# Attention plus RWKV-style FFN on 8 cores: x + attention on VectorE alone, r products moved earlier, matmuls on idle data ahead of the FFN

## The reference

```python
# x: (4, 4096, 1024) fp32; LN is layernorm without scale or shift
z = LN(x);  q, k, v = z @ Wq, z @ Wk, z @ Wv            # D = 64
att = softmax(q @ k.T, axis=1)                          # over the queries
x = x + tile(att @ v, 16)                               # the 64 columns repeated 16 times
z = LN(x);  z_prev = z shifted by one token
xr = mu_r * z + (1 - mu_r) * z_prev;  xk = mu_k * z + (1 - mu_k) * z_prev
r = sigmoid(xr @ W_r.T);  ka = square(relu(xk @ W_k.T))
x = x + r * (ka @ W_v.T)                                # W_r, W_k, W_v: 1024 x 1024
```

## Time and profile before

| | |
|---|---|
| median of 3 runs | 395.83 us (395.75 to 396.2) |
| the profiled execution | 396.79 us, span of its slowest core (core 0) 394.9 us |
| spans of the 8 cores | 388.7 to 394.9 us |
| busy: PE, DVE, ACT, POOL | 79%, 57%, 57%, 29% of the span |
| chain that ended last, by engine | PE 52%, ACT 20%, DVE 12%, issue 11% |
| costliest groups of that chain | V products (L1080) 14%, r products (L1037) 10%, keys (L1058) 10% |

### The profile page before, as it was taken

The page is one execution under the profiler, slowest core; times in us unless marked ns, Lnnn a source line. Parts: engine busy times, 40 slices in busy tenths (PEclk is TensorE's granted clock), DMA queues, the critical chain, the costliest instruction groups (busy, mean ns, idle before and its releaser), DMA issues.

```text
span 394.9 us, 6253 instructions; the slowest of 8 cores (388.7 to 394.9 us)
## 1 busy us (share of the span) xinstructions
PE 312.6 (79%) x1938; PEld 143.1 (36%) x1938; DVE 224.5 (57%) x440; ACT 225.9 (57%) x354; POOL 116.5 (29%) x161
## 2 busy tenths in 40 slices
PE   0377986696878767776526989799999999999994
PEld 0333332231224434342223334244444444444441
DVE  2787789337236631112188976879278836781045
ACT  1252289989889999999916409302860267014610
POOL 1887457607304885068470021001000000000000
PEclk9997798866695888886555989899999999999999
DMA  7999547896596789991002004131322214130014
GB/s 179 291 317 287 144 140 188 147 290 102 101 173 188 250 176 181 183 266 79 1 2 46 7 2 81 27 147 67 55 53 106 110 33 75 69 144 2 0 53 160
DMA packets 42368, 48.58 MB, mean 123 GB/s; under 512 B 33248, under 2 KB 33504, under 8 KB 41952
## 3 DMA queue, kind: packets, MB, share of 16 engines
q1 hardware_dynamic: 41472, 41.44, 37.5%
q0 software_dynamic: 864, 6.75, 10.7%
HBM read 38.68 MB, written 8.39 MB: 119 GB/s over the span
## 4 chain that ended last, share of the span: by engine, by line
PE 52%; ACT 20%; DVE 12%; issue 11%; DMA 2%; POOL 1%; DVEq 0%; SPq 0%; ACTq 0%; POOLq 0%
PE F L1080 14%; PE F L1037 10%; PE F L1058 10%; PE tf L827 6%; PE F L886 6%; ACT Prot L1139 5%; ACT junkL L1139 5%; ACT junk L1139 4%; ACT P L1139 3%; DMA xst<-x_in 2%; DVE xr L667 2%; PE acc L899 2%; PE tf L863 1%; PE tx L810 1%; DVE dxk L677 1%
## 5 line engine op out<-in xcount | busy, mean ns | idle before, releaser
L886 PE MATMUL F<-qk 64*128 64x512 bf16 x136 | 59.2, 456 | 34.4 <-ACT Prot L1139 11.0
L1058 PE MATMUL F<-dxk,wk 128*128 128x512 bf16 x256 | 58.6, 386 | 1.8 <-DVE dxk L677 1.7
L1080 PE MATMUL F<-wv,ka 128*128 128x512 bf16 x256 | 57.5, 387 | 2.9 <-ACT ka L1186 2.9
L1178 ACT ACTIVATE rr<-F 128x1024 bf16<-128x1024 f32 x16 | 16.4, 1023 | 73.6 <-PE F L1037 73.6
L1037 PE MATMUL F<-wr,xr 128*128 128x512 bf16 x256 | 57.8, 384 | 0.6 <-DVE xr L667 0.6
L890 PE MATMUL F<-qk 64*128 64x512 bf16 x120 | 54.8, 474 | 0.0
L1139 ACT ACTIVATE P<-F,negm 128x1024 bf16<-128x1024 f32 (+1 forms) x40 | 37.2, 948 | 19.5 <-PE F L886 15.6
L1139 ACT ACTIVATE junk<-F,negm 128x1024 bf16<-128x1024 f32 x32 | 39.8, 1255 | 3.1 <-PE F L890 3.1
L1139 ACT ACTIVATE junkL<-F,negm 128x1024 bf16<-128x1024 f32 x32 | 39.9, 1281 | 0.0
L417 POOL TENSOR_SCALAR zst<-xst,nmean,rstd 128x1024 bf16<-128x1024 f32 x32 | 38.0, 1194 | 3.6 <-POOL rstd L407 3.6
L1139 ACT ACTIVATE Prot<-F,negm 128x1024 bf16<-128x1024 f32 x32 | 39.0, 1346 | 0.0
(11 more groups left out here) (103 smaller groups left out, 446.7 us busy)
## 6 DMA issues: line engine op xcount, KB each, us to landing
xst<-x_in SPq DMA_DIRECT2D x32, 512.0 KB, 7.1
x<-x_in SPq DMA_DIRECT2D x16, 512.0 KB, 5.3
y_out<-x SPq DMA_DIRECT2D x15, 512.0 KB, 2.6
wr<-wr_in POOLq DMA_DIRECT2D x1, 2048.0 KB, 16.2
wk<-wk_in POOLq DMA_DIRECT2D x1, 2048.0 KB, 18.2
wv<-wv_in POOLq DMA_DIRECT2D x1, 2048.0 KB, 21.0
y_out<-x SPq DMA_DIRECT2D x2, 256.0 KB, 2.1
wqk<-wqk_in POOLq DMA_DIRECT2D x1, 256.0 KB, 9.2
```

Of the source, the lines that this page charges most:

```text
L886: t.matmul(f[:, 0:512], qk2[0:64, kt * 128:(kt + 1) * 128], qk1[0:64, i0:i0 + 512], start=True, stop=True, skip_group_check=True, tile_pos ...
L1058: ins = t.matmul(F[k_ % 3][:, dd * 512:(dd + 1) * 512], wk[:, ct, dt * 128:(dt + 1) * 128], dxk[:, q % 2, ct, :], start=(ct == 0), stop=(c ...
L1080: ins = t.matmul(F[(8 + j) % 3][:, hh * 512:(hh + 1) * 512], ka[:, dt, j * 128:(j + 1) * 128], wv2[:, dt, hh * 512:(hh + 1) * 512], start= ...
```

## The change

1. x + attention is computed by VectorE for all tiles (the table GX1, GpSimd's loop and its semaphore go). VectorE's order at the head becomes: statistics, x + attention of s = 1, the shift, then s = 0, 2, 3, and s = 4 between the first and the second mix.
2. The first statistics group takes in tiles 3 to 9 (seven instead of five), the second 10 to 15. ScalarE's copies of `acc` now come in the order tiles 3 to 7, 8 to 15, 0 to 2, VectorE waits for two of them, and `LN2OUT` is in plain order. In block 0, x + attention of s = 5 and 6 moves ahead of the second group's statistics.
3. The copy of the first turned tile out of PSUM moves from VectorE (0.69 us) to ScalarE, before `ln2_apply(2)`.
4. TensorE: all four R units of block 0 come first; behind the keys of block q comes R(q+1, 0), the next block's; R(q+1, 1), R(q+1, 2) and, for q < 2, R(q+1, 3) come behind V(q, 3). Block 3 keeps R(3, 3) behind its keys. ScalarE's sigmoids follow the same order. The `F` tiles are now handed out in turn in the order of the units (FSEQ), each free when the unit three back has been read.
5. 15 matmuls on data that is not used (`warm`) are put on TensorE: 11 before the first T2, then 1, 2 and 1 behind it.

```diff
-LN2OUT = [3, 4, 5, 6, 7, 0, 1, 2] + list(range(8, 16))
+LN2OUT = list(range(16))
...
-        LN2GRP = [(3, 8), (8, 16), (0, 3)]
+        LN2GRP = [(3, 10), (10, 16), (0, 3)]
...
-        GX1 = {1: 1, 3: 2, 4: 3}
+        X1SEQ = [1, 0, 2, 3, 4]
+        FSEQ = []
+        for q in range(4):
+            FSEQ += [("R", q, j) for j in range(1 if q else 0, 4 if q < 3 else 3)]
+            FSEQ += [("K", q, k_) for k_ in range(4)]
+            FSEQ += [("R", q + 1, 0) if q < 3 else ("R", 3, 3)]
+            FSEQ += [("V", q, j) for j in range(4)]
...
-            g.wait_ge(A_TOK, 1)
-            for s in GX1:
-                t_ = LN2SEQ[s]
-                g.wait_ge(G_XF, 4 * t_ + 4)
-                g.tensor_tensor(
-                    x1[:, t_, :], x1[:, t_, :],
-                    bass.AP(out_tok, t_ * D, [[TOWN * D, 128], [0, 16], [1, D]]),
-                    ALU.add).then_inc(G_X1, 1)
...
-            v.wait_ge(A_TOK, 1)
-            v.wait_ge(G_XF, 4 * 8)
+            v.wait_ge(A_TOK, 2)
+            v.wait_ge(G_XF, 4 * TOWN)
             ln2_stats(0)
+            ln2_x1(X1SEQ[0])
             ln2_shift(0)
...
+            def f_free(*p):
+                if f_at[p] >= 3:
+                    kind, q, i = FSEQ[f_at[p] - 3]
+                    if kind == "R":
+                        t.wait_ge(A_SIG, 4 * q + i + 1)
+                    elif kind == "K":
+                        t.wait_ge(A_RL, 4 * q + i + 1)
+                    else:
+                        t.wait_ge(V_TMP, 4 * q + i + 1)
...
+            def warm(n):
+                for i in range(n):
+                    t.matmul(F[1][:, 0:512], ident, qk2[:, 0:512], start=True, stop=True,
+                             skip_group_check=True)
+            warm(11)
             T2(1, 1, tx[1])
+            warm(1)
             T2(0, 2, tx[0])
+            warm(2)
             t.wait_ge(A_TOK, 3)
             T2(2, 3, tb[0])
-            R(0, 0)
-            R(0, 1)
-            R(0, 2)
+            warm(1)
+            for j in range(4):
+                R(0, j)
             for q in range(4):
-                if q >= 1:
-                    R(q, 0)
-                    R(q, 1)
-                    R(q, 2)
                 for k_ in range(4):
                     K(q, k_)
-                R(q, 3)
-                V(q, 0)
-                V(q, 1)
-                V(q, 2)
-                V(q, 3)
+                if q < 3:
+                    R(q + 1, 0)
+                else:
+                    R(3, 3)
+                for j in range(4):
+                    V(q, j)
...
+                if q < 3:
+                    R(q + 1, 1)
+                    R(q + 1, 2)
+                if q < 2:
+                    R(q + 1, 3)
```

More of the change, by code:

```diff
@@ L309, in build_program @@
         xk_n = lambda q: 8 + q
-        LN2GRP = [(3, 8), (8, 16), (0, 3)]
-        ln2_grp = lambda t_: 0 if 3 <= t_ < 8 else 1 if t_ >= 8 else 2
+        LN2GRP = [(3, 10), (10, 16), (0, 3)]
+        ln2_grp = lambda t_: 0 if 3 <= t_ < 10 else 1 if t_ >= 10 else 2
         x1_n = lambda q, j: 2 + 4 * q + j
         NP2 = 3
-        GX1 = {1: 1, 3: 2, 4: 3}
-        vx1_n = lambda s: s + 1 - sum(p < s for p in GX1)
+        X1SEQ = [1, 0, 2, 3, 4]
+        vx1_n = lambda s: (X1SEQ.index(s) if s < 5 else s) + 1
+        FSEQ = []
[4 more added lines that the diff above has]
+            FSEQ += [("V", q, j) for j in range(4)]
+        f_at = {p: i for i, p in enumerate(FSEQ)}
+        f_unit = lambda *p: F[f_at[p] % 3]
         t2_n = lambda s: 16 * ((s - NP2) // 2 + 1)
@@ L1027, in R @@
                     t.wait_ge(V_XR, xr_n(q, j))
[L1028 to L1032, removed]
+                f_free("R", q, j)
+                f = f_unit("R", q, j)
                 for ct in range(CT):
@@ L1048, in K @@
                     t.wait_ge(V_XK, xk_n(q) if q else 8)
[L1049 to L1052, removed]
+                f_free("K", q, k_)
+                f = f_unit("K", q, k_)
                 for dd in range(2):
@@ L1057, in K @@
                             t.wait_ge(V_XK, ct + 1)
-                        ins = t.matmul(F[k_ % 3][:, dd * 512:(dd + 1) * 512],
+                        ins = t.matmul(f[:, dd * 512:(dd + 1) * 512],
                                        wk[:, ct, dt * 128:(dt + 1) * 128],
@@ L1079, in V @@
                     dt, hh = (i % 8, i // 8) if last else (i // 2, i % 2)
-                    ins = t.matmul(F[(8 + j) % 3][:, hh * 512:(hh + 1) * 512],
+                    ins = t.matmul(f[:, hh * 512:(hh + 1) * 512],
                                    ka[:, dt, j * 128:(j + 1) * 128],
@@ L1150, in _ @@
             sc.activation(out_tok[:, 3:8, :], acc[:, 3:8, :], AF.Copy).then_inc(A_TOK, 1)
[L1151 removed]
             sc.wait_ge(P_O, KT + 1)
             sc.activation(out_tok[:, 8:16, :], acc[:, 8:16, :], AF.Copy).then_inc(A_TOK, 1)
+            sc.activation(out_tok[:, 0:3, :], acc[:, 0:3, :], AF.Copy).then_inc(A_TOK, 1)
             def ln2_apply(s):
                 t_ = LN2SEQ[s]
[L1157 to L1160 removed]
+                sc.wait_ge(V_X1, vx1_n(s))
                 sc.wait_ge(V_NM, ln2_grp(t_) + 1)
@@ L1198, in _ @@
             ln2_apply(4)
-            sig(0, 0)
-            sig(0, 1)
-            sig(0, 2)
+            for j in range(4):
+                sig(0, j)
             for q in range(4):
[L1203 to L1206, removed]
                 nx = [x1_n(q + 1, j) - 1 for j in range(4)] if q < 3 else []
@@ L1219, in _ @@
                 relu_sq(q, 3)
-                sig(q, 3)
+                if q < 3:
+                    sig(q + 1, 0)
+                    sig(q + 1, 1)
+                    sig(q + 1, 2)
+                if q < 2:
+                    sig(q + 1, 3)
+            sig(3, 3)
     return nc
```

49 lines of the change are left out of this document (20 added, 29 removed).

## The result

| | median | against before |
|---|---|---|
| before | 395.79 us (395.64 to 396.2, 4 runs) | |
| after | 393.57 us (393.11 to 394.16, 4 runs) | ratio 0.9939, 95% interval 0.992 to 0.9958 |

The change made the kernel 2.2 us faster, more than a measurement of it is uncertain. The forecast was 396.1, no change. 393.57 lies in the range and is rival (a)'s time, 393.7.

What follows compares the result with a forecast made beforehand. TensorE, never short of work from V(0, 0) on, was taken to set the end, with VectorE's chain ahead of it. Gain 3.9 us, later waits 4.2: +0.3 on 395.83 gives 396.1; own range 394.8 to 397.0, whole range 393.3 to 397.8.

Steps and rivals of the forecast that it cites:

- rival (a): R(1, 0) runs at full clock, as keys end later or the restart is quick: 2.4 us back, 393.7; chance 0.20.
- The head: VectorE's start of the FFN: without GpSimd's additions, statistics take 3.45 us and nmr comes 3.8 us earlier.
- rival (d): VectorE's slow first statistics come from something other than GpSimd, so 4.9 us stay: 401.0; chance 0.06.
- the straight line: GpSimd's power over six tiles, scaled from three and eight tiles without lock: 1.9 us, ending at 234.6; 235.1 was taken.
- R(0, 1) to the keys' end: TensorE in block 0: R(0, 1) at 215.4, three r units and four keys at 3.45 us each, ending at 239.6.
- The 2.4 us at R(1, 0): TensorE idles 239.6 to 245.1 and restarts at 1.2 GHz for 4.8 us, half lost; bounds 1.1 to 3.3.
- What is late next: New waits before R(2, 0), R(3, 0) and K(3, 0): losses of 1.47, 1.27 and 1.47, together 4.2 us.
- Rival (c): Waits of R(2, 0) and R(3, 0) are absent because ScalarE's z comes earlier: 2.8 us less, 393.3; chance 0.08.
- (b): The three later waits each let the clock fall, 1.65 us apiece: one gives 397.8, three 401.1; chance 0.12.
- The sum: Loss of 4.2 less gain of 3.9 at V(0, 0) makes +0.3 us, 396.1 on the median.

Runs made afterwards that it cites:

- Kernel 8: The kernel before, with GpSimd's three additions held until VectorE's first statistics are done: 395.5 us, ratio 0.9974.
- kernel 1: The changed kernel without its 15 matmuls on unused data: 395.95 us, ratio 0.9997 to before.
- 4: The changed kernel with 8 more matmuls on idle data between R(0, 0) and R(0, 1), filling the wait there: 395.89 us, ratio 1.0000 to before.
- kernel 5: The changed kernel without its 15 matmuls, but with 18 idle matmuls between K(0, 3) and R(1, 0): 393.46 us, ratio 0.992 to before.
- kernel 9: New head, old unit order, no idle matmuls, with first statistics over five tiles instead of seven: 394.37 us, ratio 0.9963 to before.
- kernel 3: The kernel before with only the new order of units and sigmoids, old head, no idle matmuls: 401.57 us, ratio 1.0135.
- 11: Kernel 9 with ScalarE's first three relus of block 0 ahead of the first z of block 1: 392.55 us, ratio 0.9923 to before.
- 2: The changed kernel with the old order of units and no idle matmuls, so the new head alone: 386.78 us, ratio 0.9763 to before.

## Why the prediction was wrong

- **The head** was right as far as VectorE goes. Statistics began at 198.58 and took 3.45 us to 202.03 (forecast 3.45), nmr 203.47 (203.8, or 203.2 with the 0.6), first mix 207.82 (208.25), mix_k 220.79 (221.3), power's end 234.43 (235.1), first mix_d of block 1 239.40 (240.3), start of R(1, 0) 244.33 (245.1). The Trainium skill (SBUF — State Buffer, "SBUF: two separate sides") says that an instruction of VectorE with two SBUF inputs and one of GpSimd lock each other out. By it the power would end at 234.5, by the straight line at 234.06; it ended at 234.43. Kernel 8 shows the lock by itself, with VectorE's additions at 3.33 us beside GpSimd's and 1.22 alone; rival (d) is out.
- **R(0, 1) to the keys' end is the step that failed.** I wrote that the keys "end at 239.6" and that "a clock that they keep up buys nothing on the path, since behind R(0, 0) TensorE waits for VectorE anyway". I costed the low clock only where the path runs, and let TensorE go through the slack ahead of it at full pace. A fast R(0, 0) makes the wait at R(0, 1) 2.2 us long, and the clock fell there. It cost 1.7 us of slack (12.04 against 10.36), ended the keys later by as much, and so shortened the idle time before R(1, 0) from 5.0 to 3.3 us. Behind 5.0 us the clock was low in all eight cores (kernels 1 and 4), behind 3.3 in two of eight (after), behind 1.1 in none (kernel 5).
- **The 2.4 us at R(1, 0)** were right for the kernel without the idle matmuls: 5.98 - 3.61 = 2.37 in kernel 1, and the low stretch, 6.8 us, began about 2 us before the restart. In after they did not fall due in the slowest core; in cores 0 and 5 R(1, 0) took 5.30 us, 1.7 lost. This is rival (a), by the first of its two reasons, "the keys end later than I think". I gave it 0.20 because I compared 5.5 us of idle time with 2.85 and never asked what the 15 matmuls would do to the 5.5.
- **What is late next** was right: 1.47, 1.27 and 1.47 forecast, from start to start. Measured so, the delays are 1.41, 1.42 and 1.61 (287.31 - 272.09, 330.17 - 314.94 and 355.96 - 347.44, less 13.81 for 64 matmuls and 6.91 for 32); the brackets show 1.25, 1.26 and 1.45. Rival (c) is out. So is (b): behind those waits the clock was full. The Trainium skill (TensorE: Matmul & The Clock Gate, "Why this matters for your kernels") asks for no gap above about 3 us; for these three it agrees. Elsewhere the traces differ from it on both sides: the clock fell behind 2.21 us at R(0, 1), and stayed full behind 3.29 us at R(1, 0) in core 4 and behind 3.86 us at V(0, 0) in core 2 of kernel 9.
- **The sum.** V(0, 0) at 247.78 instead of the equivalent 254.87, less 0.6 us of earlier attention, is a gain of 6.5; less 4.4 for the later waits it leaves 2.1, and the medians differ by 2.2. (The profiled executions differ by 2.6, with the 0.6 of attention in it.) Forecast was a loss of 0.3. The one term of 2.4 us is the whole miss.

What I did not see at all, though the trace of before held it, is that the two halves of the change work against each other. I read V(0, 0)'s wait for `ka` as a fixed thing that the new order has to go around. It was ScalarE's z standing in front of the relus, and the head removes it with the seven tiles of its first group, so that the reordering had nothing left to gain and its waits to pay. With the old head it gains nothing either (kernel 3): it gives up a wait of 2.85 us for one of 7.49.

## What to carry to other kernels

Work that fills idle time ahead of slack is not free of effect because the slack takes it up: it changes how long the next wait is, and with that where TensorE's clock falls. Follow the clock through the slack, not only along the path, and if a low clock on the path is the cost, put the filling right ahead of it (kernel 5), where its effect does not hang on a chain of chances. Before reordering units around a wait, look up what the waited-for engine had in front of the missing piece, and try each half of a change alone: here one half gained 9 us and the other cost most of it.

## What was unexpected of the hardware

The same idle time does not always do the same to the clock. In kernel 9 all eight cores waited 3.85 or 3.86 us at V(0, 0), behind the same work; cores 1, 2, 3 and 5 stayed at 2.4 GHz, cores 0, 4, 6 and 7 fell to 1.2. Core 2, then core 7:

```profile
247.57 13.97 PE L1080 MATMUL F<-wv,ka 128*128 128x512 bf16 x63 [3.86 <-ACT ka L1181]
```
```profile
242.61 15.66 PE L1080 MATMUL F<-wv,ka 128*128 128x512 bf16 x64 [3.86 <-ACT ka L1181]
```

In the changed kernel six cores waited 3.29 to 3.31 us at R(1, 0) and kept the clock, and the two that waited 3.34 and 3.35 us lost it (core 5):

```profile
244.00:247.00 3.00, 3.00 (x8) 1.06 (x7) 2.90 (x8) 0.00 (x0) 0.00 (x0) 0.50 0.00 0
```

A 4.98 us wait made a low stretch of 6.8 us in all eight cores, waits of 1.25 to 1.46 us none; waits of 2.2 us at R(0, 1) made one of 3.4 us in every core of the changed kernel. Between 1.9 and 3.9 us these runs show both. The single wait before it is not all that counts, either. In before the clock fell for 3.4 us in all eight cores among the first keys, where TensorE waits six times for 0.29 us, and 57 matmuls took 14.04 us:

```profile
229.43 14.04 PE L1058 MATMUL F<-dxk,wk 128*128 128x512 bf16 x57 [0.29 <-DVE dxk L677]
```

It fell there in all eight cores of 9 and 11 too, and in none of 2, with the same six waits. In before this lies in slack, since V(0, 0) waits for `ka` all the same; in 2 it would have been on the path, so some 1.7 us of the head's gain was neither forecast nor tried by itself. What decides between two cores, or two kernels, with the same waits was not tried.
